# Three sets of key sums of a graph transformer's mixing part change place with the last qkv product

## The chip, the cores and the metric

The kernel runs on 1 core of a Trainium2 chip. The metric is the device time of one execution in microseconds. Where several runs are given, their median counts. The engines are PE (matmuls), DVE, ACT and POOL (elementwise work, POOL here above all as the issuer of scattering DMAs), and SP, which only issues DMAs.

## What is computed

A layer over a graph with 3125 nodes of 256 features: a layer norm, then a three-layer graph convolution and a mixing part side by side, their sum, and a feed-forward block for half of the nodes.

```python
xn = _layernorm(x)
x = x + gnn(xn, edge_index, ...) + mix(xn[None], ...)[0]
x = x + ffn(_layernorm(x)[None], ...)[0]
```

The change lies in the mixing part. With one position in the sequence its attention over the nodes comes down to elementwise work and small products:

```python
h = conv1d(logmap0(proj(x)), w_qkv)            # 256 -> 768 channels
t = logmap0(proj(expmap0(relu(batchnorm(h)))))
s = pointwise(depthwise(t))                    # "spread": 768 -> 768, groups of 32
q, k, v = split(concat(t, s))                  # per group of 96 channels
out = q * sum_over_group(k * v) / v            # "key sums" and quotients
ft = conv1d(out_on_the_ball, w_res) + b_res
```

The reference writes `vk = einsum(v, k)`, `out = einsum(vk, q)` and divides by the sum of `v`; for length 1 and 32 channels a group, a key sum of 32 channels is the only sum across channels in it.

## The kernel before

**Two parts that run against each other.** POOL issues 416 scattering DMAs (L763), four a row over 104 rows of edges, that build the matrix of edge counts in DRAM tile by tile. Meanwhile the other engines do the mixing part, in five chunks of 5 x 125 nodes (`NC` = 5, chunk `c`). Then PE begins with the first layer of the graph convolution. For each of 25 tiles SP waits until POOL's scatters for that tile have landed (`landed`), fetches the tile of counts into a ring of four slots (`fetch`), and PE multiplies it with the rows (`aggregate1`). POOL waits for the mixing part in some rows (`mixing_kept_up`: `qk_done` and `sq_done` by `KEYS_BY_ROW` and `SQUARES_BY_ROW`). Row 37 waits for the last key product of chunk 3.

**One turn of the mixing loop on PE** (L2452 to L2489, chunk `c`). The order is written out by hand; each engine works its own list in that order, and semaphores tie the lists together:

- first and second key sums of chunk `c`, with the output sums and residual products of chunk `c - 1` between and behind them (`outs`, `outs_turned`, `outs_rest`);
- six qkv products of chunk `c + 1`, `hidden(c + 1, m)` with `m` from 0 to 5. Each goes to one of two pairs of PSUM banks. ACT copies it out with a ReLU and squares it (L1821, L1814). From `m` = 2 on, a product waits until ACT has copied out the one two before it (`h_done`), so the last one, `m` = 5, waits for ACT's copy of 3. Behind products 3 and 5, `hidden` also issues a pair of norm sums over the squares (`norm_pair`);
- third and fourth key sums of chunk `c`, `key_sums(c, 2)` and `key_sums(c, 3)`, somewhere among the products;
- six spread products of chunk `c + 1`, `spread(c + 1, m)`, copied and squared by ACT (L1831, L1814), with norm sums between, then the last norm sums, ACT's copy of them (L1842) and their spread over the partitions (`norm_spread`).

A set of key sums is two matmuls with the block matrix `kones` into banks 6 and 7. The trace shows each fp32 matmul as two, so four in all. It waits for the product before it in the same banks (`qk_done`) and for ACT's copies of the spread (`s_evac`):

```python
def key_sums(c, n):
    ...
    for h in range(2):
        last = mm(bank(6 + h, 128, CH), kones[:, :], src[:, 2 + half, h * CH:(h + 1) * CH], True, True)
    last.then_inc(sem("k_done"), 1)
```

**Who waits for it.** DVE, in `key(c, n)` (L1219), multiplies q with the sums and signals `qk_done`. Its list for a chunk ends with: quotients of the second half (six elementwise passes, a reciprocal of 4.07 us, two more), `key(c, 3)`, `weigh(c, 2)`, `weigh(c, 3)`, then what `besides(c, 5)` puts there: one-hot batches for the node degrees in chunks 0 and 1, low halves of four weight pieces and twelve rows in chunk 3. The first key product of the next chunk follows. ACT squares the weighed outputs late, after its `veps_made` (`out_square`), and PE's output sums wait for that.

In the timelines, `psum<-big,wm` or `psum<-scr,wm` in f16 with x12 is a qkv product, in f32 spread products (x4 for one), `psum<-...,kones` key sums, `psum<-...,ones` with 128*32 norm sums (313 columns) or output sums (375 columns), `psum<-acc` bf16 degree batches, and `psum<-rows,scr` an aggregate of layer 1. L2164 is the helper that issues every matmul.

Of the kernel before, what the change touches and what calls it, by code (L numbers as in the profile page):

```python
# [144 lines left out]
def _build(ctx, nc, a, out, scratch):  # L145
# [7 lines left out]
    def sem(name):  # L153
        if name not in sems:
            sems[name] = ctx.enter_context(nc.semaphore(name))
        return sems[name]

    def milestone(name):

        if name in PE_MILESTONES:  # L160
            return sem("pe_milestones")
        return sem("act_milestones" if name in ACT_MILESTONES else "dve_milestones")
# [257 lines left out]
    def bank(b, p, n, o=0):  # L420
        return psum[:p, b, o:o + n]
# [1740 lines left out]
    def _(pe):  # L2162
        def mm(o, l, r, start, stop):
            return pe.matmul(o, l, r, start=start, stop=stop)  # L2164
# [31 lines left out]
        def degree(b):  # L2196
            ohp, oht = onehot[HOME[b]]
            pe.wait_ge(sem("onehot_done"), b + 1)
            if b == DEGREE_RUNS[0]:
                pe.wait_ge(sem("ft_done"), G)  # L2200
            for j in range(DB):
                last = mm(psum[TW * (j % 4):TW * (j % 4) + TW, 5, 0:P], oht[:, j // 2, :, j % 2],
                          ohp[:, j // 2, :, j % 2], b in (0, DEGREE_RUNS[0]) and j < 4,
                          b in (DEGREE_RUNS[0] - 1, sum(DEGREE_RUNS) - 1) and j >= DB - 4)
            last.then_inc(sem("degree_used"), 1)
# [79 lines left out]
        def bias_product():  # L2285
            pe.wait_ge(sem("layerw_loaded"), 48)
            pe.wait_ge(sem("cols_loaded"), 80)
            pe.wait_ge(sem("ft_done"), (NC - 1) * G)
            for k in range(8):
                last = mm(bank(5, P, D2), free(be1c[:, k:k + 1], 0, [[0, P]]), w2[:, k, :], k == 0, k == 7)  # L2290
            last.then_inc(milestone("be2w_done"), 1)

        def degrees_and_bounds():
            pe.wait_ge(sem("degree_kept"), 2)
            pe.wait_ge(milestone("squares_summed"), AFTER["squares_summed"])
            mm(bank(5, 128, 7, 16), ones[:, :], sums7, True, True).then_inc(milestone("bounds_done"), 1)
            mm(bank(5, P, T, 256), degree4, quarters, True, True).then_inc(milestone("degree_summed"), 1)
# [14 lines left out]
        def norm_spread(c):  # L2312
            pe.wait_ge(sem("norm_kept"), c + 1)
            pe.wait_ge(sem("s_evac"), c * NT + NT)
            pe.wait_ge(sem("sq_done"), c * 12 + 12)
            if c == 0:
                pe.wait_ge(sem("chosen_ready"), 4)
            for h in range(2):
                last = mm(bank(h, 128, CH), chosen[:, h, :], sums_kept, True, True)
            last.then_inc(sem("norm_spread"), 1)  # L2320

        def hidden(c, m):
            if m >= 2:
                pe.wait_ge(sem("h_done"), c * NT + (m - 1))
            elif c >= 1:
                pe.wait_ge(sem("row_kept"), c)
                pe.wait_ge(sem("s_evac"), c * NT + (m - 1))
                pe.wait_ge(sem("sq_done"), c * 12 + (m - 1))
                if c >= 2:
                    pe.wait_ge(sem("ft_done"), (c - 2) * G + 2 * m + 2)  # L2330
            for k in range(2):
                for hx, hw in ((0, 0), (1, 0), (0, 1)):
                    for h in range(2):
                        o = c * CW + h * CH
                        last = mm(bank(2 * (m % 2) + h, 128, CH), wq16[:, k, 1 - hw, m * 128:(m + 1) * 128],
                                  z16[:, k, hx, o:o + CH], k == 0 and (hx, hw) == (0, 0), k == 1 and (hx, hw) == (0, 1))
            last.then_inc(sem("qkv_done"), 1)
            if m in (3, 5):
                norm_pair(c, m // 2 - 1)
# [16 lines left out]
        def part_of(c, n):  # L2356
            return (hTs[c % 2], n) if n < 2 else (sTs[c % 2], n - 2)

        def key_sums(c, n):
            src, half = part_of(c, n)  # L2360
            pe.wait_ge(sem("qk_done"), c * 4 + n)
            if c == 0 and n == 0:
                pe.wait_ge(milestone("needs_ready"), AFTER["needs_ready"])
                pe.wait_ge(milestone("value_kept"), AFTER["value_kept"])
            if n >= 2:
                pe.wait_ge(sem("s_evac"), c * NT + n + 1)
# [3 lines that stand above are left out]
# [9 lines left out]
        def outs(c):  # L2379
            newest = min(c + 1, NC - 1)  # L2380
            pe.wait_ge(sem("osq_done"), c * 4 + 4)
            pe.wait_ge(sem("norm_kept"), newest + 1)
            for n in range(4):
                src, half = part_of(c, n)
                for h, (lo, hi) in enumerate(OUTS):
                    last = mm(quarter(2 * (n % 2) + h, 3 * P), ones[:, 0:32], src[:, 2 + half, lo:hi], n < 2, n >= 2)
            last.then_inc(sem("out_summed"), 1)
            pe.wait_ge(sem("o_done"), c * 4 + 4)
            pe.wait_ge(sem("row_kept"), newest + 1)
            pe.wait_ge(sem("s_evac"), newest * NT + NT)  # L2390
            pe.wait_ge(sem("sq_done"), newest * 12 + 12)
            if c >= 1:
                pe.wait_ge(sem("ft_done"), c * G)
            for j in range(AHEAD[c]):
                res(c, j)

        def outs_rest(c):

            for j in range(AHEAD[c], G):
                if j == 4 and c == 0:  # L2400
                    pe.wait_ge(sem("degree_kept"), 1)
                if j == 4 and c == 1:
                    pe.wait_ge(milestone("dinv_read"), AFTER["dinv_read"])
                    pe.wait_ge(milestone("bounds_read"), AFTER["bounds_read"])
                if j == 3 and c == NC - 1:
                    pe.wait_ge(milestone("be2w_read"), AFTER["be2w_read"])
                if j == 4 and c == NC - 1:
                    pe.wait_ge(sem("ft_done"), T - G + 1)
                res(c, j)

        def outs_turned(c):
            pe.wait_ge(sem("out_kept"), c + 1)
            for j in range(G):
                pe.transpose(bank(4, P, 1, 440 + j), umax_row[c % 2][:, j * P:(j + 1) * P], ident[0:1, 0:1])
            for j in range(G):
                o = j * P if j < 3 else j * P - OUTS[1][0]
                last = mm(bank(4, P, 1, 432 + j), outs_kept[:, o:o + P], chosen[:, j // 3, 0:1], True, True)
            last.then_inc(sem("out_turned"), 1)

        def degrees(c, at):  # L2420
            for b in range(*HALF_BATCHES[c][at]) if c < len(HALF_BATCHES) else ():
                degree(b)
# [29 lines left out]
        for c in range(NC):  # L2452
            key_sums(c, 0)
            if c >= 1:
                outs(c - 1)
            if c == 2:
                degrees_and_bounds()
            if c >= 1:
                outs_turned(c - 1)
            if c == 0:  # L2460
                for b in range(3, EARLY):
                    degree(b)
            key_sums(c, 1)
            if c >= 1:
                outs_rest(c - 1)
            degrees(c, 0)
            if c == NC - 1:
                key_sums(c, 2)
                bias_product()
                key_sums(c, 3)  # L2470
                break
            for m in range(NT):
                hidden(c + 1, m)
                if m == (0 if c else 3):
                    key_sums(c, 2)
                if m == 4 and c >= 1:
                    key_sums(c, 3)
                for b in range(*BETWEEN.get((c, m), (0, 0))):
                    degree(b)
            if c == 0:  # L2480
                key_sums(c, 3)
            spread(c + 1, 0, 3)
            if c == 0:
                degrees(c, 3)
            spread(c + 1, 3, NT)
            norm_pair(c + 1, 5)
            norm_spread(c + 1)
            degrees(c, 4)
            degrees(c, 5)  # L2489
# [363 lines left out]
```

## Time and profile before

| | |
|---|---|
| time, median of 3 runs | 1286.18 us (1285.31 to 1288.14) |
| the profiled execution | 1287.64 us, span 1285.8 us |
| PE busy | 1183.7 us (92%), 6591 matmuls |
| DVE busy | 732.1 us (57%) |
| POOL busy | 567.9 us (44%), 444.3 us of it in the 416 scatters |
| ACT busy | 478.9 us (37%) |
| granted clock of PE, mean | 0.979 |

The mixing loop lies between some 107 and 325 us of the span, layer 1 of the convolution from there to about 700 us, layers 2 and 3 behind it. POOL scatters from 95.85 us to 674 us. A row of a timeline gives the start, the time from the first start to the last end of what it merges, engine, line, operation, output and inputs, how many, and in brackets the idle time before it with what ended it. Rows of one engine can overlap a little, since a matmul's drain is in its duration. So the price of a piece of PE's list is read from start to start.

### The profile page before, as it was taken

How to read it: one execution, taken by the hardware profiler on the slowest of the kernel's cores; microseconds unless marked ns; L12 is line 12 of the kernel's file. 1: busy time of each engine (PE TensorE's matmuls, PEld its weight loads, DVE VectorE, ACT ScalarE, POOL GpSimd, SP SyncE). 2: the span in 40 equal slices, each digit the busy share in tenths (PEclk: the TensorE clock that was granted, in tenths of full speed). 3: DMA queues.
4: the chain of work that ended last, by engine and by line, in shares of the span. 5: the costliest groups of instructions: out<-in, count | busy, mean ns of one | idle time of the engine just before them, and what ended most of it. 6: DMA issues, size and time to landing. Idle time of an engine off the chain costs nothing.

```text
span 1285.8 us, 19145 instructions
## 1 busy us (share of the span) xinstructions
PE 1183.7 (92%) x6591; PEld 780.0 (61%) x6591; DVE 732.1 (57%) x1560; ACT 478.9 (37%) x1028; POOL 567.9 (44%) x580
## 2 busy tenths in 40 slices
PE   2998799889999999999979999999999899996995
PEld 2765456556665666666645666666666566653674
DVE  7878997779555455545523343333323388887253
ACT  4546873886432222223211123111111144441463
POOL 4108887777777777777773400440000000000633
PEclk9989898999999999999989999999999999998998
DMA  9882000004223221211314064333333266523201
GB/s 266 285 269 77 1 1 2 2 1 110 73 72 91 71 57 31 54 37 49 78 33 102 1 187 107 96 86 79 93 84 82 77 176 170 166 69 120 54 19 34
DMA packets 82939, 111.30 MB, mean 87 GB/s; under 512 B 51871, under 2 KB 67348, under 8 KB 82872
## 3 DMA queue, kind: packets, MB, share of 16 engines
q1 hardware_dynamic: 62344, 106.98, 30.2%
q0 software_dynamic: 20528, 3.47, 1.9%
q8 instruction: 37, 0.61, 0.2%
q14 instruction: 30, 0.25, 0.1%
HBM read 76.08 MB, written 27.67 MB: 81 GB/s over the span
## 4 chain that ended last, share of the span: by engine, by line
PE 48%; POOL 24%; issue 19%; DVE 6%; ACT 2%; DMA 1%; POOLq 1%; SPq 0%; DVEq 0%; ACTq 0%
PE psum L2164 47%; POOL counts L763 23%; ACT acc L1706 1%; POOLq L763 1%; DMA scr<-counts 0%; DVE scr L1562 0%; DVE big L965 0%; DVE scr L965 0%; DMA scr<-in_src_pad 0%; PE psum L2544 0%; DVE col L885 0%; POOL col L742 0%; PE psum L2702 0%; POOL out L822 0%; DVE big L958 0%
## 5 line engine op out<-in xcount | busy, mean ns | idle before, releaser
L763 POOL DMA_INDIRECT counts<-big,eidx x416 | 444.3, 1068 | 164.3 <-issue 127.9
L2164 PE MATMUL psum<-big,scr 125*125 125x512 f16 x1250 | 278.2, 382 | 7.2 <-DVE big L1362 6.5
L2164 PE MATMUL psum<-rows,scr 125*125 125x512 f16 x1250 | 274.6, 379 | 6.2 <-DMA scr<-counts 2.6
L2164 PEld LDWEIGHTS psum<-rows,scr 125*125 125x125 f16 x1250 | 170.1, 136 | 106.2 <-DMA scr<-counts 3.5
L2164 PEld LDWEIGHTS psum<-big,scr 125*125 125x125 f16 x1250 | 171.0, 138 | 104.6 <-DVE big L1362 7.0
L2164 PE MATMUL psum<-wb,scr 128*125 128x512 f16 x600 | 138.4, 382 | 2.4 <-DVE scr L1345 1.9
L2164 PEld LDWEIGHTS psum<-wb,scr 128*125 128x125 f16 x600 | 81.6, 137 | 48.3 <-issue 2.3
L815 POOL DMA_INDIRECT scr<-picked,eidx x13 | 22.9, 1758 | 181.0 <-issue 181.0
L1345 DVE TENSOR_TENSOR scr<-psum,scr 128x1000 f16<-128x1000 f32 x25 | 30.0, 1200 | 89.3 <-ACT scr L1989 89.1
L2164 PE MATMUL psum<-big,wm 128*128 128x313 f16 (+1 forms) x432 | 74.8, 324 | 3.1 <-ACT scr L1821 1.5
L1441 DVE SCALAR_TENSOR_TENSOR scr<-psum,col,wm 125x512 f32<-125x512 f32 x25 | 18.7, 749 | 98.8 <-PE psum L2164 98.8
L869 DVE BATCH_NORM_STATS2 col<-scr 125x6 f32<-125x512 f32 x75 | 49.5, 689 | 44.1 <-ACT scr L1998 28.1
L2164 PE MATMUL psum<-wa,scr 128*125 128x512 f16 x300 | 69.0, 379 | 2.4 <-DVE scr L1240 1.8
L804 POOL IOTA scr<- 125x63 f32 x1 | 0.2, 202 | 159.9 <-PE psum L2164 159.9
L2060 ACT ACTIVATE scr<-scr 125x512 f32<-125x512 f32 x25 | 15.7, 629 | 135.3 <-DVE scr L1441 135.3
L2164 PEld LDWEIGHTS psum<-big,wm 128*128 128x128 f16 (+1 forms) x432 | 47.7, 114 | 28.3 <-issue 5.4
L2164 PEld LDWEIGHTS psum<-wa,scr 128*125 128x125 f16 x300 | 40.6, 136 | 26.6 <-DVE scr L1240 2.7
L1989 ACT CAST scr<-psum 128x1000 f16<-128x1000 f32 x25 | 24.8, 992 | 70.2 <-PE psum L2164 56.2
L795 POOL TENSOR_SCALAR scr<-wa,col 128x512 f32<-128x512 f32 x4 | 6.3, 1587 | 100.9 <-DVE col L1467 100.6
L1993 ACT ACTIVATE big<-scr,col 125x512 f32 (+1 forms) x25 | 18.0, 722 | 80.4 <-DVE scr L1358 80.4
L1213 DVE RECIPROCAL scr<-scr 128x626 f32<-128x626 f32 x10 | 40.7, 4066 | 0.3
L822 POOL DMA_INDIRECT out<-rows,eidx x13 | 23.1, 1780 | 40.0 <-issue 30.6
(419 smaller groups left out, 1861.7 us busy)
## 6 DMA issues: line engine op xcount, KB each, us to landing
scr<-counts SPq DMA_DIRECT2D x75, 683.6 KB
counts<-wb SPq DMA_DIRECT2D x25, 683.6 KB
counts<-big,eidx POOLq DMA_INDIRECT x416
scr<-counts SPq DMA_DIRECT2D x75, 79.3 KB
scr<-in_x SPq DMA_DIRECT2D x25, 125.0 KB
picked<-big SPq DMA_DIRECT2D x5, 566.6 KB
rows<-in_x SPq DMA_DIRECT2D x5, 560.0 KB
out<-acc SPq DMA_DIRECT2D x5, 560.0 KB
```

Source lines behind the costliest of these rows:

```text
L763: pool.indirect_dma_start(cells, bass.IndirectOffsetOnAxis(ap=eidx[:, r * EQ + g:r * EQ + g + 1], axis=0), evalue[:, at_c:at_c + 1], None, ...
L815: pool.indirect_dma_start(got[:, g, :], None, picked_dram, bass.IndirectOffsetOnAxis(ap=picked[:, g:g + 1], axis=0), bounds_check=N - 1, o ...
L822: pool.indirect_dma_start(out, bass.IndirectOffsetOnAxis(ap=picked[:n, g:g + 1], axis=0), base[:n, g, :], None, bounds_check=N - 1, oob_is ...
L869: done.did(dve.bn_stats(st2[:, h, :], src[:, h * 512:(h + 1) * 512] if parts > 1 else src))
L1213: done.did(dve.reciprocal(tdiv, tdiv))
L1345: dve.tensor_tensor(xT16[:, 1].rearrange("p (b k) q -> p b (k q)", b=2), turned_halves(), xT16[:, 0].rearrange("p (b k) q -> p b (k q)", b ...
L1441: dve.scalar_tensor_tensor(out=pre[b][:, 0:D2], in0=bank(home, P, D2), scalar=d2out[:, bass.ds(t, 1)], in1=b2r, op0=ALU.mult, op1=ALU.add) ...
L1706: act.activation(zv[:, t, 0:D], x_rows[:, t, :], ACT.Identity, scale=z_scale[:, t:t + 1], bias=z_shift[:, t:t + 1]).then_inc(sem("z_done"), 1)
L1989: act.copy(xT16[:, 0].rearrange("p (b k) q -> p b (k q)", b=2), turned_halves()).then_inc(sem("xThi_done"), 1)
L1993: act.activation(h2in[:, t, 0, :], hbuf, ACT.Identity, scale=h2_scale[:, bass.ds(t, 1)]).then_inc(sem("hi2_done"), 1)
L2060: act.activation(pre[b][:, 0:D2], pre[b][:, 0:D2], ACT.Relu).then_inc(sem("relu2_done"), 1)
L2164: return pe.matmul(o, l, r, start=start, stop=stop)
```

## The change

In chunks 1, 2 and 3 `key_sums(c, 3)` moves from behind `hidden(c + 1, 4)` to behind `hidden(c + 1, 5)`, where chunk 0 has it already. In chunk 1 two degree batches (20 and 21) stood between the key sums and the last product; they now follow product 4 directly. Nothing is added or removed, and the lists of the other engines are untouched.

```diff
                 if m == (0 if c else 3):
                     key_sums(c, 2)
-                if m == 4 and c >= 1:
-                    key_sums(c, 3)
                 for b in range(*BETWEEN.get((c, m), (0, 0))):
                     degree(b)
-            if c == 0:
-                key_sums(c, 3)
+            key_sums(c, 3)
             spread(c + 1, 0, 3)
```

PE's list in chunk 1, from the product in front of the two changed places to the first spread products (here and below, `kones` are key sums, `acc` degree batches, `ones` norm sums, `wm` x12 a qkv product and `wm` x4 two spread products):

```order
 L2164 MATMUL psum<-acc 32x125 x32
 L2164 MATMUL psum<-big,wm 128x313 x12
-L2164 MATMUL psum<-scr,kones 128x313 x2
 L2164 MATMUL psum<-acc 32x125 x32
 L2164 MATMUL psum<-big,wm 128x313 x12
 L2164 MATMUL psum<-big,ones 32x313 x2
 L2164 MATMUL psum<-scr,ones 32x313 x2
+L2164 MATMUL psum<-scr,kones 128x313 x2
 L2164 MATMUL psum<-big,wm 128x313 x4
```

The key sums moved past two degree batches, the last product and the four matmuls of its norm sums.

PE's list in chunk 2 (chunk 3 reads the same but for the names of the buffers):

```order
-L2164 MATMUL psum<-big,wm 128x313 x12
-L2164 MATMUL psum<-scr,kones 128x313 x2
-L2164 MATMUL psum<-big,wm 128x313 x12
-L2164 MATMUL psum<-big,ones 32x313 x2
-L2164 MATMUL psum<-scr,ones 32x313 x2
+L2164 MATMUL psum<-big,wm 128x313 x24
+L2164 MATMUL psum<-big,ones 32x313 x2
+L2164 MATMUL psum<-scr,ones 32x313 x2
+L2164 MATMUL psum<-scr,kones 128x313 x2
 L2164 MATMUL psum<-scr,wm 128x313 x4
```

Products 4 and 5 now stand in a row (x24), their norm sums behind them, and the key sums last, right before the spread products.

## Rows read from the trace of the kernel before

**Rows 1.** the page's chain of waits, shares of the span by engine

```profile
PE 48%; POOL 24%; issue 19%; DVE 6%; ACT 2%; DMA 1%; POOLq 1%; SPq 0%; DVEq 0%; ACTq 0%
```

**Rows 2.** the chain in order of time: start us, us, what

```profile
638.24 0.13 POOL col L742
...
638.74 5.68 DMA scr<-counts
```

**Rows 3.** timeline of PE from 620: start, us, what [idle before <-releaser]

```profile
623.58 5.61 PE L2164 MATMUL psum<-rows,scr 125*125 125x512 f16 x25 [1.31 <-DMA scr<-counts]
...
644.46 5.61 PE L2164 MATMUL psum<-rows,scr 125*125 125x512 f16 x25 [1.25 <-DMA scr<-counts]
...
665.42 7.12 PE L2164 MATMUL psum<-big,scr 125*125 125x512 f16 x18 [6.51 <-DVE big L1362]
```

**Rows 4.** one stretch: us, busy us by engine (instructions), PEclk, DMA share, GB/s

```profile
402.00:622.00 220.00, 219.80 (x1099) 145.11 (x1099) 113.49 (x200) 61.18 (x107) 167.52 (x179) 1.00 0.22 54
```

**Rows 5.** timeline of PE, chunk 2

```profile
225.56 1.22 PE L2164 MATMUL psum<-scr,kones 128*128 128x313 f32 x4
228.23 1.79 PE L2164 MATMUL psum<-big,wm 128*128 128x313 f16 x12 [1.46 <-ACT scr L1821]
...
230.62 2.38 PE L2164 MATMUL psum<-scr,wm 128*128 128x313 f32 x8
...
240.42 0.46 PE L2164 MATMUL psum<-big,ones 128*32 128x313 f32 x2 [0.82 <-ACT scr L1814]
...
246.63 0.84 PE L2164 MATMUL psum<-big,ones 128*32 128x375 f32 x8 [2.56 <-ACT scr L1838]
```

**Rows 6.** timeline of ACT, chunk 2

```profile
227.32 0.86 ACT L1821 ACTIVATE scr<-psum,col 128x626 f32<-128x626 f32 x1
...
231.98 0.69 ACT L1831 ACTIVATE scr<-psum 128x626 f32<-128x626 f32 x1
```

**Rows 7.** timeline of all engines, chunk 0

```profile
125.55 1.32 PE L2164 MATMUL psum<-scr,kones 128*128 128x313 f32 x4
...
126.71 2.27 PE L2164 MATMUL psum<-scr,wm 128*128 128x313 f32 x8
...
127.96 0.69 ACT L1831 ACTIVATE scr<-psum 128x626 f32<-128x626 f32 x1 [1.53 <-PE psum L2164]
```

**Rows 8.** timeline of all engines, chunk 1

```profile
178.44 0.86 ACT L1821 ACTIVATE big<-psum,col 128x626 f32<-128x626 f32 x1
...
179.36 1.79 PE L2164 MATMUL psum<-big,wm 128*128 128x313 f16 x12
...
181.74 2.38 PE L2164 MATMUL psum<-big,wm 128*128 128x313 f32 x8
```

**Rows 9.** timeline of DVE, chunks 1 to 4

```profile
191.17 0.81 DVE L1197 SCALAR_TENSOR_TENSOR scr<-psum,scr 128x626 f32<-128x626 f32 x1
...
234.21 0.81 DVE L1197 SCALAR_TENSOR_TENSOR scr<-psum,scr 128x626 f32<-128x626 f32 x1
...
272.98 0.81 DVE L1197 SCALAR_TENSOR_TENSOR scr<-psum,scr 128x626 f32<-128x626 f32 x1
...
288.21 0.81 DVE L1197 SCALAR_TENSOR_TENSOR big<-psum,big 128x626 f32<-128x626 f32 x1 [6.06 <-PE psum L2164]
```

**Rows 10.** timeline of DVE, then of POOL

```profile
278.05 4.11 DVE L1197 SCALAR_TENSOR_TENSOR rows<-big,rows 125x256 f16<-125x256 f32 x12
...
278.62 4.38 POOL L763 DMA_INDIRECT counts<-big,eidx  x1 [0.31 <-issue]
...
320.66 0.97 POOL L763 DMA_INDIRECT counts<-big,eidx  x1 [0.70 <-issue]
```

**Rows 11.** stretches around two hand-overs, columns as in group 4

```profile
190.00:197.00 7.00, 3.82 (x69) 1.73 (x68) 5.88 (x8) 4.70 (x8) 5.48 (x6) 1.00 0.03 3
197.00:204.00 7.00, 6.34 (x38) 2.78 (x39) 4.63 (x15) 1.18 (x3) 5.68 (x6) 0.51 0.02 0
239.00:246.00 7.00, 3.72 (x24) 1.63 (x20) 1.82 (x3) 4.70 (x9) 5.29 (x8) 1.00 0.03 4
```

## The prediction

> **What bounds the kernel now.** I read the page's chain of waits first, then the chain in order of time. A quarter of the chain is POOL, almost all of it the 416 scatters at L763 [rows 1]. In order of time the chain leaves POOL at 638.24 us. SP then fetches a tile of counts, whose DMA runs from 638.74 for 5.68 us, and PE starts on it at 644.46 [rows 2, 3]. From there to the end PE carries most of the chain. So the instant that fixes the second half is 644.46, and two runners race for it: POOL, which scatters without pause, and PE, which comes out of the mixing part (the part that is changed) and then works through layer 1.
>
> The timeline of PE between 620 and 670 us says who loses. PE stood still for 1.31 us before 623.58 and for 1.25 us before 644.46, both times until a DMA of counts landed [rows 3]. Between 402 and 622 us PE was busy for 219.80 of 220.00 us [rows 4], so the lag with which it comes out of mixing is still there at 622. PE therefore has 1.31 + 1.25 = 2.56 us to spare at 644.46. **Up to 2.56 us that PE loses in mixing costs nothing, and nothing that PE wins there counts**, unless POOL's landings move too.
>
> POOL does have waits on the mixing part, so its slack must be read. The scatter row that waits for the last key product of chunk 3 starts at 320.66 [rows 10], while DVE starts that product at 272.98 [rows 9]. That is 47.7 us of slack, and no delay discussed here is near it.
>
> **What PE does at the changed places.** Take chunk 2. The key sums start at 225.56. Then PE is idle for 1.46 us and the last qkv product starts at 228.23, released by ACT [rows 5]: its semaphore asks for ACT's copy of product 3 (they count from 0), which runs from 227.32 for 0.86 us [rows 6]. The key sums fill a hole that ACT leaves anyhow. With them gone the hole is larger by their time, and the product starts where it started. So the product gains nothing. Chunk 3 repeats this 44.1 us later with the same 1.46 us. In chunk 1 the hole is filled: the product starts at 179.36, but ACT's copy of product 3 starts only at 178.44 and takes 0.86 us, so it is free at 179.30 [rows 8]. There too the product gains 0.06 us at most.
>
> **What the key sums cost in their new place.** They now stand between the norm sums behind the last product and the first spread product. The kernel before has this very order once, in chunk 0: key sums at 125.55, spread at 126.71 [rows 7]. That is 1.16 us for one set, with its weight loads. In chunks 1 to 3 PE goes from that spread to the last norm sums without a hole (230.62 to the one before 240.42 in chunk 2, which ACT ends [rows 5]), so the 1.16 us isn't filled up on PE. What could swallow part of it is ACT, which copies the first spread. In chunk 2 the copy starts at 231.98 with no idle time before it [rows 6], 1.36 us after the spread, so ACT is just not waiting. In chunk 0 the copy starts 127.96 - 126.71 = 1.25 us after the spread [rows 7]. In the new order the spread of chunk 2 starts at 230.62 + 1.16 = 231.78 and the copy at 233.03, so 1.05 us late. A chunk thus loses between 1.05 and 1.16 us. All that follows to the hand-over of the chunk (the last squares, the sums, their spread, the output sums that wait until 246.63) hangs on this pair of engines and moves with it. **Three chunks: 3.15 to 3.48 us, taken as 3.3.**
>
> **Does the later key sum hold up DVE?** k_done now comes when the moved sums end, 1.32 us after their start [rows 7]. Chunk 1: 181.74 + 1.32 = 183.06 [rows 8], and DVE takes that key product at 191.17 [rows 9], behind quotients and one-hot batches. No wait. Chunk 2: 230.62 + 1.32 = 231.94, DVE at 234.21 [rows 5, 9]. Covered with 2.3 us. Chunk 3: 44.1 us after chunk 2, at 276.04, against 272.98 before: **here DVE waits 3.1 us.** Queued behind it are two weighings, the four low weight pieces and twelve rows (the block at 278.05, 4.11 us [rows 10]). Behind that DVE sat idle for 6.06 us before 288.21, until PE's first key sums of chunk 4 [rows 9]. 3.1 fits into 6.06, so it costs nothing. If that cover were gone it would cost up to 3.1 us. POOL's wait on it has the 47.7 us named above.
>
> **The sum.** Work added or removed: none. PE leaves mixing 3.3 us late. It keeps this lag through layer 1, where its waits before 622 us are for engines that follow it. Of the lag 1.31 is swallowed at 623.58 and 1.25 at 644.46: 3.3 - 2.56 = 0.7. With the ends of the terms it is 0.6 to 0.9; I take 0.8, nearer the price of the chunk-0 row, which is the same piece of order. The next wait, 6.51 us before 665.42, is for DVE's rows that come out of PE's own product after 644.46 [rows 3], so it moves along. The profiled execution took 1287.64 us for a span of 1285.8; it would become 1288.4. It lies 1.46 above the median of the three runs, 1286.18, on which I build: **1287.0 us**, +0.06%. A measurement of this kernel can tell about 0.2% (2.6 us) from no change.
>
> **Rivals.**
> 1. *No trace at all.* PE's clock was granted at 1.00 from 190 to 197 us, with PE busy for 3.82 of 7.00 us, and at 0.51 (1.2 GHz, the lower of its levels) in the 7 us behind [rows 11]. Busy 6.34 us at 0.51 is work of some 3.3 us, so this fall costs about 3.0 us. The change moves work by about 1.1 us against it. If the fall stays away, PE's lag is 3.3 - 3.0 = 0.3 and POOL's landing decides as before: 1286.2. PE alone could then be at most 2.56 - 0.3 = 2.3 us earlier, and only if POOL too came earlier by as much.
> 2. *Slower, by the clock.* The hand-over from chunk 2 to 3 looks much like that first one: 3.72 us busy from 239 to 246, yet the clock stayed at 1.00 [rows 11]. In the new order it comes 2.2 us later. If the clock falls there as it did at 197, the price is another 3.0: 3.3 + 3.0 - 2.56 = 3.7, so 1289.9. It decides from the point where the lag exceeds 2.56 + 2.6 us. Against it: the holes of both late hand-overs passed at full clock. The Trainium skill, "TensorE: Matmul & The Clock Gate", section on the HAM clock gate, says that the throttled clock is the default and that activity releases it, which makes the wider hole before the last product (2.6 us instead of 1.46) a risk too; by that rule alone the change would lose in three more places. The trace shows holes of 2.56 us, as before 246.63 [rows 5], with the clock at 1.00, so here it is no more than a chance.
> 3. *The spare time isn't there.* One scatter took 4.38 us at 278.62 where its neighbours take 1.3, just under DVE's block of twelve rows at 278.05 [rows 10]. The change moves that block by 2.2 + 3.1 = 5.3 us against POOL. If a scatter slips in between the rows, POOL is up to 3.4 us earlier, the two waits for landings vanish, and the whole 3.3 is paid: 1289.5. If two are caught, POOL is later and the end with it, by less than that. The Trainium skill, "SBUF — State Buffer", section "SBUF: two separate sides", says that DVE and GpSimd share one port pair as an exclusive lock, taken by whoever starts first, and that DMAs issued from GpSimd starve for it. By that rule the block catches one scatter wherever it lands, or misses by a hair; the trace agrees with the long scatter, and no row shows how often it misses.
> 4. *Faster.* It needs rival 1 and an earlier POOL together, and even then gives 2.3 us, under the bound. Only with noise on top does it pass 0.2%.
> 5. *The change does nothing.* Excluded by the order: the two matmuls stand elsewhere in three chunks.
>
> **How the numbers follow.** Forecast (1286.8 to 1287.1 before noise) 0.60. Rival 1: 0.15. Rival 2: 0.11. Rival 3: 0.10, half of it above the bound of 0.2%. Rival 4: 0.04. Within 0.2%: 0.60 + 0.15 + 0.05 = 0.80. Slower: 0.11 + 0.05 = 0.16. Faster: 0.04. The three runs before spread from 1285.3 to 1288.1, which the range must carry under the forecast and rival 1. Above, it reaches to rivals 2 and 3: 1285.2 to 1289.9.
>
> **What would show it.** In the trace after: the last product starts at the same distance from ACT's copy of product 3, with an idle of about 2.6 us before it in chunks 2 and 3. The key sums follow, and the first spread starts 1.16 us later in each of three chunks. DVE idles some 3 us before the last key product of chunk 3 and that much less before chunk 4. PE enters layer 1 about 3.3 us later, and its two waits for counts shrink to nothing. The forecast is wrong if the lag at layer 1 is under 2 or over 4.5 us, if the granted clock falls somewhere new, or if PE still waits over 0.5 us for counts.

## The result, and the profile after

**The kernel after is slower, and slower than the prediction's range.** Over six runs each: after 1293.22 us median (1289.50 to 1296.17), before 1287.21 (1285.31 to 1288.14), ratio 1.0047 with a 95% interval of 1.0033 to 1.0061. That is 4 to 8 us, where 0.8 was forecast. The profiled execution of after is the lowest of its runs: 1289.50 us, span 1287.7, mean granted clock 0.975 against 0.979. Its trace therefore shows less than the usual loss.

The page's chain of waits has lost its POOL part, [rows 1] had 24% there:

```profile
PE 80%; DVE 10%; ACT 5%; issue 2%; DMA 2%; POOL 0%; DVEq 0%; SPq 0%; ACTq 0%; POOLq 0%
```

Below, product 4 and product 5 are the last two of the six qkv products, and the hand-over to a chunk is the stretch between its first and second set of key sums, in which the output sums of the chunk before it are made. Timeline of PE in chunks 2 and 3, in layer 1 and behind it, after:

```profile
223.01 1.79 PE L2164 MATMUL psum<-big,wm 128*128 128x313 f16 x12
227.32 1.79 PE L2164 MATMUL psum<-big,wm 128*128 128x313 f16 x12 [2.51 <-ACT scr L1821]
...
230.86 2.27 PE L2164 MATMUL psum<-scr,wm 128*128 128x313 f32 x8
...
268.16 1.79 PE L2164 MATMUL psum<-big,wm 128*128 128x313 f16 x12
272.46 2.70 PE L2164 MATMUL psum<-big,wm 128*128 128x313 f16 x12 [2.51 <-ACT big L1821]
...
277.57 2.28 PE L2164 MATMUL psum<-big,wm 128*128 128x313 f32 x8
...
309.69 1.32 PE L2164 MATMUL psum<-scr,kones 128*128 128x313 f32 x4 [1.29 <-DVE big L1197]
...
645.78 5.56 PE L2164 MATMUL psum<-rows,scr 125*125 125x512 f16 x25
...
666.44 7.08 PE L2164 MATMUL psum<-big,scr 125*125 125x512 f16 x18 [6.26 <-DVE big L1362]
...
760.96 1.52 PE L2164 MATMUL psum<-wc,scr 128*125 128x256 f16 x12 [0.87 <-DMA scr<-scr]
```

The kernel before has this row where after has the one at 309.69:

```profile
305.30 1.32 PE L2164 MATMUL psum<-scr,kones 128*128 128x313 f32 x4 [1.29 <-DVE big L1197]
```

Chunk 2 is what the prediction drew: a hole of 2.51 us, product 5 in 1.79 us, 7.85 us from product 4 to the first spread product (before 6.69, so 1.16 more). Chunk 3 has the same hole, but behind it product 5 takes longer, and from product 4 to the spread it is 277.57 - 268.16 = 9.41 us, **1.56 more than in chunk 2**. The windows say why (start and end us, length, busy us of PE, its weight loads, DVE, ACT and POOL with their instructions, then the granted clock and the DMA's share and rate), after first, then before:

```profile
272.00:276.00 4.00, 3.54 (x20) 1.59 (x20) 1.08 (x2) 3.42 (x5) 3.08 (x4) 0.64 0.02 2
...
292.00:296.00 4.00, 2.51 (x16) 0.59 (x16) 3.93 (x6) 3.50 (x7) 3.39 (x3) 0.70 0.02 0
```

```profile
272.00:276.00 4.00, 3.67 (x25) 2.24 (x26) 3.90 (x6) 3.90 (x6) 3.12 (x3) 1.00 0.02 2
...
292.00:296.00 4.00, 4.00 (x22) 3.14 (x19) 3.96 (x3) 3.97 (x10) 3.20 (x5) 1.00 0.01 0
```

The granted clock is 0.64 and 0.70, a mix of 1.2 and 2.4 GHz, in two stretches where the kernel before has 1.00. The second lies in the hand-over to chunk 4, behind a hole of 2.56 us that both orders have. On the other hand the fall of [rows 11] at 197 us is gone in this execution. At 309.69 PE is 4.39 us behind before (305.30). At 645.78 1.32 us of this are left ([rows 3]: 644.46), at 666.44 1.02, and PE no longer waits for counts. A wait of 0.87 us for a transposing DMA at 760.96, where before had none, doubles that, and the span ends 1.9 us later.

### The profile page after: what moved, and what is told of

Read it like the earlier page. It is cut to its first block, busy times and chain, and to the rows that moved or that the text cites. A ratio compares the mean times of both kernels' runs of the same rounds, so it can differ in the third digit from the quotient of the medians.

```text
span 1287.7 us, 19145 instructions
## 1 busy us (share of the span) xinstructions
PE 1185.4 (92%) x6591; PEld 780.4 (61%) x6591; DVE 731.5 (57%) x1560; ACT 479.1 (37%) x1028; POOL 567.8 (44%) x580
## 4 chain that ended last, share of the span: by engine, by line
PE 80%; DVE 10%; ACT 5%; issue 2%; DMA 2%; POOL 0%; DVEq 0%; SPq 0%; ACTq 0%; POOLq 0%
PE psum L2164 78%; PE psum L2541 2%; DVE acc L944 1%; DMA scr<-scr 1%; DVE scr L1197 1%; DVE scr L1213 1%; DVE big L1197 1%; ACT acc L1706 1%; DMA scr<-picked,eidx 1%; ACT scr L1989 0%; PE psum L2534 0%; ACT scr L1831 0%; DVE acc L946 0%; ACT scr L1857 0%; DVE big L965 0%
## 5 line engine op out<-in xcount | busy, mean ns | idle before, releaser
L1441 DVE SCALAR_TENSOR_TENSOR scr<-psum,col,wm 125x512 f32<-125x512 f32 x25 | 18.6, 749 | 98.8 <-PE psum L2164 98.8
```

Of the source, the lines that this page charges most:

```text
L1441: dve.scalar_tensor_tensor(out=pre[b][:, 0:D2], in0=bank(home, P, D2), scalar=d2out[:, bass.ds(t, 1)], in1=b2r, op0=ALU.mult, op1=ALU.add) ...
```

## The experiments

**Two theories.** A, the clock: the wider holes before product 5 make PE's granted clock fall, and each fall is paid because the lag is already beyond the cover. B, the lag: the later key sums cost 1.16 us a chunk or more, further down too, and the falls are incidental. The kernel that tells them apart keeps the new order and puts matmuls whose result nobody uses into the two holes ("filled" below; an idle time of 1.40 us is left, about the 1.46 of before). All experiments but the unchanged ones are edits of one loop.

**The conditions.** In 16 of the 18 runs the kernel before, timed beside them, took 1455 to 1467 us and not 1288. The engines, PE above all, stood still there for longer in front of instructions for which the profile names no releaser. It reads as if the instructions themselves came late, which no run shows. The same kernel after, its PE weight loads' idle time in the view of waits (total us, times, longest), then the stretch from 140 to 180 us, first in the profiled execution above, then in f1_after:

```profile
PEld psum L2164 <- issue: 51.7, 140, 1.8
...
140.00:180.00 40.00, 32.27 (x346) 21.54 (x344) 35.63 (x49) 31.99 (x82) 32.31 (x29) 0.87 0.02 2
```

```profile
PEld psum L2164 <- issue: 111.7, 259, 2.6
...
140.00:180.00 40.00, 24.06 (x150) 10.35 (x153) 18.95 (x21) 12.68 (x22) 24.49 (x25) 0.66 0.02 1
```

PE began 150 matmuls against 346 in these 40 us. It stood still for 15.9 us of them in f1_after, 12.3 without a releaser; the program is also at a later place in after by then. What brings this about is open. It is not the chip: it struck five chips, and h1_before to h3_late had it on the same one as i1_after and i2_fill, half an hour apart from them, had not. Two runs, i1_after and i2_fill, met the conditions of the result and decide on time. The others are used for what their traces show at product 5, and only weakly for time: there POOL has no share in the page's chain, so no lag is covered, and the intervals are 0.3 to 0.5% to each side.

### The order of after with filled holes: e1_fill, f2_fill, g1_fill, i2_fill

Against after (the kernel has the loop in a helper, here it is written out):

```diff
             for m in range(NT):
                 hidden(c + 1, m)
...
+                if m == 4 and c >= 2:
+                    for _ in range(5):
+                        mm(bank(5, 128, 128, 300), kones[:, :], ident[:, :], True, True)
...
             key_sums(c, 3)
```

> The new order, with five idle 128x128 matmuls (result unused, kones by ident, into a spare place of bank 5) between products 4 and 5 of chunks 2 and 3, where the kernel after lets PE stand for 2.51 us. They fill the hole and leave the order and its lag as they are. Theory A (clock): the wider holes make the granted clock fall more often, in the profiled execution of after at 274 us and then at 294; most of the 6 us are such falls. Filled, the fall at 274 goes, and the time is before plus 1 to 3 us (lag 3.3 less the 2.56 of cover, and what is left of the falls). Theory B (lag): PE's list simply comes late and the late start is paid in full or more downstream; the filler changes nothing, before plus 6 us.

> The new order with the holes of 2.51 us before product 5 of chunks 2 and 3 filled with five matmuls of unused result, as in e1_fill. Where before takes some 1287 us, theory A (clock): before plus 1 to 3 us, no clock fall between 265 and 290 us. Theory B (lag): before plus 6 us, as f1_after.

> The same kernel as e1_fill and f2_fill (new order, holes of 2.51 us in chunks 2 and 3 filled with matmuls of unused result), on its own. The question is first whether before takes 1287 us or 1455 us beside it. At 1287: theory A (clock) before plus 1 to 3 us, theory B (lag) before plus 6 us, the loss of after. At 1455: PE is held up for want of instructions in the mixing part, the holes are elsewhere, and neither theory expects more than 4 us.

> The new order with filled holes once more. If before takes 1287 us beside it: theory A (clock) 1288 to 1290, 3 to 5 us under the kernel after; theory B (lag) the same as after, 1293. If before takes 1455 to 1470 us again: product 5 at 1.79 us in both chunks by theory A, and a time between those of before and after.

### The kernel after once more: f1_after, h2_after, i1_after

> The kernel after once more, unchanged, to have its time beside the experiments and a second trace of it. On a chip where before takes some 1287 us: both theories 1291 to 1295; theory A (clock): granted clock 0.004 to 0.006 under that of before in the timed executions and, in the trace, the falls at 272 and 292 us again or others in the mixing part. Theory B (lag): the clock is as in before and the lag at layer 1 is over 4 us all the same. On a chip like that of the first four experiments (before 1456 us, PE held up for want of instructions) POOL ends no chain, so no lag is covered: before plus 3 to 6 us by either.

> The kernel after, unchanged. So far the traces of the new order show product 5 longer than 2.3 us (full clock: 1.79) in 6 of the 7 places where a hole of over 2.1 us stands before it, and in none of the 15 places with a narrow or filled hole. Theory A (clock): the product is slowed again in chunks 2 and 3 wherever the hole is over 2.1 us. From product 4 to the first spread product it then takes 9.3 to 9.5 us in place of 7.85. Time: before plus 2 to 6 us, if PE's want of instructions leaves such holes. Theory B (lag): 7.85 us in both chunks, and all of the time's loss is the order's 1.16 us per chunk: before plus 3.3.

> The kernel after once more. If before takes 1287 us beside it: after 1291 to 1296 by both theories; theory A (clock) expects in its trace one fall of the clock more than in the profiled execution, at the hand-over from chunk 1 to 2 or before product 5 of chunk 2, in executions that take 1293 us. If before takes 1455 to 1470 us again: two more holes before product 5, slowed (over 2.0 us in place of 1.79) by theory A where they are over 2.1 us wide.

**Measured, i1_after and i2_fill** (same chip, one comparison, before 1288.01 us median): after 1291.79 us, ratio 1.0029 (1.0017 to 1.0040); filled 1286.70 us, ratio 0.9993 (0.9981 to 1.0006). The loss is there again and **filling the holes takes all of it away, 5.1 us between the medians**, although the key sums still stand late and PE executes 20 matmuls more. Theory A expected 1288 to 1290 for the filled kernel, theory B 1293: it came in under both, far nearer to A.

The scatter of the 7 and 12 executions puts 3.1 to 6.4 us around the difference of the means, 4.8 us (an estimate from their times). The granted clock says the same for all of them and not only for the profiled ones: 0.9749 on average in after, 0.9787 filled, 0.9774 in the 18 of before. 0.0038 of 1290 us are 4.9 us (an estimate), so the clock is the size of the whole difference. Late instructions are not: PE's own idle time without a releaser is 1.6 us in before, after, i1_after and i2_fill alike.

The traces show where, PE in i1_after (its profiled execution is the highest of its 7, 1293.68 us):

```profile
224.92 1.79 PE L2164 MATMUL psum<-big,wm 128*128 128x313 f16 x12
229.22 2.39 PE L2164 MATMUL psum<-big,wm 128*128 128x313 f16 x12 [2.51 <-ACT scr L1821]
...
234.34 2.27 PE L2164 MATMUL psum<-scr,wm 128*128 128x313 f32 x8
...
273.29 1.79 PE L2164 MATMUL psum<-big,wm 128*128 128x313 f16 x12
277.59 2.93 PE L2164 MATMUL psum<-big,wm 128*128 128x313 f16 x12 [2.51 <-ACT big L1821]
...
282.74 2.27 PE L2164 MATMUL psum<-big,wm 128*128 128x313 f32 x8
...
314.77 1.32 PE L2164 MATMUL psum<-scr,kones 128*128 128x313 f32 x4 [1.29 <-DVE big L1197]
...
671.53 6.98 PE L2164 MATMUL psum<-big,scr 125*125 125x512 f16 x18 [6.27 <-DVE big L1362]
...
707.86 7.08 PE L2164 MATMUL psum<-wb,scr 128*125 128x512 f16 x24 [1.89 <-DVE scr L1345]
```

and in i2_fill:

```profile
224.72 1.79 PE L2164 MATMUL psum<-big,wm 128*128 128x313 f16 x12
226.35 1.28 PE L2164 MATMUL psum<-ident,kones 128*128 128x128 f32 x10
229.03 1.79 PE L2164 MATMUL psum<-big,wm 128*128 128x313 f16 x12 [1.40 <-ACT scr L1821]
...
232.58 2.27 PE L2164 MATMUL psum<-scr,wm 128*128 128x313 f32 x8
...
269.88 1.79 PE L2164 MATMUL psum<-big,wm 128*128 128x313 f16 x12
271.50 1.28 PE L2164 MATMUL psum<-ident,kones 128*128 128x128 f32 x10
274.18 1.79 PE L2164 MATMUL psum<-big,wm 128*128 128x313 f16 x12 [1.40 <-ACT big L1821]
...
277.73 2.27 PE L2164 MATMUL psum<-big,wm 128*128 128x313 f32 x8
...
309.84 1.32 PE L2164 MATMUL psum<-scr,kones 128*128 128x313 f32 x4 [1.29 <-DVE big L1197]
...
666.60 5.87 PE L2164 MATMUL psum<-big,scr 125*125 125x512 f16 x18 [6.26 <-DVE big L1362]
...
701.82 5.39 PE L2164 MATMUL psum<-wb,scr 128*125 128x512 f16 x24 [1.89 <-DVE scr L1345]
```

From product 4 to the first spread product it is 9.42 and 9.45 us in i1_after, 7.86 and 7.85 in i2_fill: each fall costs 1.6 us. The product starts 4.30 or 4.31 us after product 4 in both kernels; the filler moves nothing, it only keeps PE at work. The clock of 272 to 280 us, i1_after first:

```profile
272.00:276.00 4.00, 3.08 (x26) 1.53 (x23) 3.97 (x2) 3.62 (x12) 3.09 (x4) 1.00 0.02 2
276.00:280.00 4.00, 2.41 (x11) 1.47 (x12) 2.17 (x3) 3.75 (x6) 3.09 (x4) 0.76 0.01 0
```

```profile
272.00:276.00 4.00, 2.60 (x23) 1.78 (x26) 2.76 (x3) 3.94 (x8) 3.09 (x4) 1.00 0.01 0
276.00:280.00 4.00, 4.00 (x24) 2.32 (x28) 1.97 (x3) 2.91 (x5) 3.09 (x4) 1.00 0.02 0
```

The end of mixing (309 to 315 us) comes 314.77 - 309.84 = 4.9 us apart: 1.6 + 1.6 for the two products, and 1.6 for the hand-over to chunk 3, where i1_after has a fall and i2_fill none. In the hand-over to chunk 4 both have one (12.12 and 12.20 us in place of 10.57). At 666 us it is still 4.9. Two stages behind it are 1.1 and 1.7 us shorter in the filled kernel (the last two rows of each; before has the long form at 701.89 too); 0.9 of that is lost at once to a wait for DVE. 4.9 + 1.1 + 1.7 - 0.9 = 6.8, the difference of the spans (1291.9 and 1285.1). So of this one pair 4.9 us come out of mixing, and 1.9 lie in stages whose clock happened to fall otherwise; no hole of the change is near them.

**Measured, the others.** Filled: 1.0018 (0.9986 to 1.0050), 1.0009 (0.9976 to 1.0042), 1.0011 (0.9981 to 1.0041). After: 0.9986 (0.9946 to 1.0027), 1.0014 (0.9985 to 1.0044). Where before takes 1455 us and more, neither differs measurably from it. The 3 to 6 us that f1_after's expectation named are not confirmed, and only half excluded. But their traces have the falls: product 5 takes 3.28 us in chunk 3 of f1_after and 3.32 and 2.08 us in chunks 2 and 3 of h2_after. It is slowed in none of the six places of the three filled ones. In two of these, chunk 2 of e1_fill and of f2_fill, product 4 was late and no wide hole would have stood there, so four of the six test the filler.

### Before, only chunk 1, only chunks 2 and 3: h1_before, e2_only1, j4_only1, e3_only23, f3_only23, j1_only23

Against before:

```diff
-                if m == 4 and c >= 1:
+                if m == 4 and c >= 1 and c not in (2, 3):    # (1,) for "only chunk 1"
                     key_sums(c, 3)
...
-            if c == 0:
+            if c == 0 or c in (2, 3):                        # (1,)
                 key_sums(c, 3)
```

> The kernel before, unchanged, for a trace of it under the conditions of these runs (some 1455 us), and as a test of the comparison with itself: ratio 1 within its interval. Theory A (clock): product 5 of chunks 2 and 3 stands behind holes of at most 1.9 us and takes 1.79 us in both, the duration at full clock. Theory B (lag) has no view of that.

> Only chunk 1 has the new order; there the place in front of product 5 is filled by degree batches in either order, so no hole grows. Theory A (clock): within 1 us of before, unless the hand-over from chunk 1 to 2, where the clock of before is at 0.51 from 197 to 204 us, keeps its clock as it did in the profiled execution of after; then PE enters layer 1 some 2 us earlier and POOL's landings hold the time where it was. Theory B (lag): 1.1 us of lag is under the 2.56 us of cover, so 0; if instead every chunk's move costs alike, before plus 2 us.

> Only chunk 1 in the new order, where no hole grows, beside a before of some 1288 us. Both theories: 1.16 us of lag under the cover: within 1 us of before. If it were over 2 us slower, chunk 1 would carry a part of the loss that neither explains.

> Only chunks 2 and 3 have the new order; both get the hole of 2.51 us. Theory A (clock): both wide holes are there, so most of the loss is: before plus 4 to 6 us, with the clock falling between 270 and 300 us. Theory B (lag): 2.3 us of lag is under the 2.56 us of cover, so 0 to 0.5 us; if every chunk's move costs alike, before plus 4 us.

> Only chunks 2 and 3 in the new order, as in e3_only23. Where before takes some 1287 us, theory A (clock): before plus 3 to 6 us, with falls of the clock between 265 and 300 us. Theory B (lag): 2.3 us of lag is under the 2.56 us of cover, so 0 to 0.5 us.

> Only chunks 2 and 3 in the new order, beside a before of some 1288 us. Theory A (clock), with the sizes of the second trace of after (1.55 us per slowed product 5, 1.5 us per slowed hand-over behind it): lag 2 x 1.16 + 2 x 1.55 + up to 2 x 1.5, less the 2.6 to 3.1 us of cover: before plus 3 to 5 us. Theory B (lag alone): 2.3 us, less than the cover: before plus 0 to 0.5 us.

**Measured.** Before against itself 0.9989 (0.9963 to 1.0016). Only chunk 1: 1.0006 (0.9973 to 1.0039) and 1.0021 (0.9989 to 1.0052). Only chunks 2 and 3: 1.0034 (0.9998 to 1.0071), 1.0015 (0.9970 to 1.0059), 1.0015 (0.9978 to 1.0052). All three of the latter lean to the slow side and none is measurable alone; as times they settle nothing. The traces do. f3_only23 in chunk 3, and h1_before in chunk 3:

```profile
345.27 2.36 PE L2164 MATMUL psum<-big,wm 128*128 128x313 f16 x12 [2.51 <-ACT big L1821]
```

```profile
343.67 1.79 PE L2164 MATMUL psum<-big,wm 128*128 128x313 f16 x12
...
347.97 1.79 PE L2164 MATMUL psum<-big,wm 128*128 128x313 f16 x12 [1.45 <-ACT big L1821]
```

### Late matmuls without a wide hole: e4b_lag, f4_lag, j2_lag

Against before (again written out):

```diff
             if c == 0:
                 key_sums(c, 3)
+            if c >= 2:
+                for _ in range(8):
+                    mm(bank(5, 128, 128, 300), kones[:, :], ident[:, :], True, True)
             spread(c + 1, 0, 3)
```

> The order of before, its holes as narrow as they were (1.46 us), and eight idle 128x128 matmuls (result unused) behind the last product's norm sums in chunks 2 and 3, some 1.7 us each: a lag of about 3.4 us without a wide hole. Theory A (clock): the lag less the cover, before plus 0.8 to 2 us. Theory B (lag): the same loss as after, before plus 6 us.

> The order of before with 2 x 1.7 us of matmuls of unused result behind product 5 of chunks 2 and 3, as in e4b_lag. Where before takes some 1287 us, theory A (clock): before plus 0.8 to 2 us, clock as in before. Theory B (lag): before plus 6 us, as f1_after.

> The order of before with 2 x 1.7 us of matmuls of unused result behind product 5 of chunks 2 and 3, beside a before of some 1288 us. Theory A (clock): a lag of 3.4 us with narrow holes, so before plus 0 to 1 us, like the filled kernel. Theory B (lag): the loss of after, plus 4 to 6 us.

**Measured.** 1.0052 (1.0021 to 1.0083), 1.0033 (0.9994 to 1.0072), 0.9991 (0.9951 to 1.0031). Inconclusive between the theories: a lag of 3.4 us without any cover is 0.23%, and 6 us are 0.41%; of the three intervals the first two hold both and the last holds only the smaller. Product 5 ran in 1.79 us in all six places, so none of them has a fall there. This never ran beside a before of 1288 us.

### The key sums later still: h3_late, j3_late

Against after:

```diff
-            key_sums(c, 3)
+            if c == 0:
+                key_sums(c, 3)
...
             spread(c + 1, 3, NT)
+            if c >= 1:
+                key_sums(c, 3)
             norm_pair(c + 1, 5)
```

> The key sums of chunks 1 to 3 moved still further back, behind the last spread product's norm sums and before the last norm sums, where PE waits 0.82 us for ACT in any case. The hole of 2.51 us before product 5 stays, but the spread products no longer start 1.16 us late. Theory A (clock): product 5 of chunks 2 and 3 is slowed as in the kernel after; before plus 2 to 4 us. Theory B (lag): only some 0.4 us of lag per chunk is left; no difference to before.

> The key sums behind the last spread product, holes of 2.51 us before product 5 and 0.4 us of lag per chunk, beside a before of some 1288 us. Theory A (clock): two to four falls of 1.5 us each, 3 to 6 us, plus 1.2, less 3 us of cover: before plus 1 to 4 us. Rival C, from the earlier trace of this kernel, in which both products 5 ran at full clock behind holes of over 2.5 us: the hole alone does not do it, and the time is that of before.

**Measured, a miss for all.** 1.0080 (1.0044 to 1.0115) and 1.0162 (1.0112 to 1.0212): 12 and 24 us, far more than any theory had. In h3_late mixing isn't where they go. The stretches to 400 and to 550 us and PE's idle time without a releaser, h1_before and then h3_late:

```profile
0.00:400.00 400.00, 291.04 (x1857) 182.11 (x1858) 262.65 (x444) 202.17 (x396) 223.04 (x232) 0.88 0.28 81
0.00:550.00 550.00, 397.72 (x2329) 249.32 (x2329) 316.02 (x542) 237.04 (x465) 306.73 (x320) 0.86 0.25 72
...
PE psum L2164 <- issue: 29.0, 40, 2.3
```

```profile
0.00:400.00 400.00, 297.44 (x1863) 186.16 (x1864) 264.73 (x447) 201.93 (x396) 219.72 (x225) 0.87 0.28 82
0.00:550.00 550.00, 399.01 (x2303) 248.39 (x2304) 311.28 (x534) 235.34 (x463) 304.37 (x315) 0.85 0.25 72
...
PE psum L2164 <- issue: 47.6, 47, 6.7
```

At 400 us PE has begun 1863 matmuls against 1857; at 550 us, in layer 1, 2303 against 2329, and over the whole span it stood without a releaser for 18.6 us longer. Why this order brings it about wasn't taken apart; as a time the experiment says nothing on the two theories. Against the simplest form of theory A, that every wide hole brings a fall, stands what PE did in h3_late:

```profile
347.18 1.79 PE L2164 MATMUL psum<-big,wm 128*128 128x313 f16 x12 [2.51 <-ACT big L1821]
```

Behind holes of 2.89 and 2.51 us both products ran at full clock. A wide hole alone is not enough.

### Product 5 in all traces

| before product 5 of chunks 2 and 3 | places | longer than 1.79 us |
|---|---|---|
| idle 2.20 to 2.89 us, key sums moved away | 15 | 12 |
| idle of at most 1.83 us (before's order, filled, or narrow by chance) | 25 | 0 |

The 15 are: both places of after, i1_after, h2_after, e3_only23, f3_only23 and h3_late, and chunk 3 of f1_after, j1_only23 and j3_late. The three at full clock are chunk 2 of after and both of h3_late. The table counts every trace, before's own included. One of the 12 doesn't belong to its hole: in chunk 2 of e3_only23 product 4 already took 3.32 us, behind a wait of 4.74 us, and the clock stayed at 0.50 through the 2.23 us before product 5. So 11 of 14 places lost the clock in the hole itself. Against them stand the six filled places with the same 4.30 us from product 4 to product 5 (both of g1_fill and i2_fill, chunk 3 of e1_fill and f2_fill): none of the six was slowed. The hand-over to chunk 4, whose hole is 2.56 us in either order, slowed its output sums in 9 of 13 traces with chunk 3 in the new order and in 2 of 7 in the old one, the hand-over to chunk 3 in 8 of 13 and in 3 of 7: a lean, not a proof. A slowed product 5 is not what it needs: of the 9, 5 followed one (of 8 slowed) and 4 did not (of 5), and three of the four filled kernels are among these 4.

## Why the prediction was wrong

**The sum for the order was right.** 1.05 to 1.16 us a chunk: product 4 to the first spread product went from 6.69 to 7.85 us, 1.16, with the clock undisturbed. That is the upper end of the range, 3.48 us for three where 3.3 was taken. The product itself gained nothing: it starts 4.30 or 4.31 us after product 4 in before, after and filled alike, with 2.51 us of idle time in after where 2.6 was forecast.

**DVE's part was right.** It waited before the last key product of chunk 3 (after):

```profile
277.84 0.81 DVE L1197 SCALAR_TENSOR_TENSOR scr<-psum,scr 128x626 f32<-128x626 f32 x1 [4.76 <-PE psum L2164]
...
290.96 0.81 DVE L1197 SCALAR_TENSOR_TENSOR big<-psum,big 128x626 f32<-128x626 f32 x1 [3.95 <-PE psum L2164]
```

4.76 us in place of 3.1, the slowed product being in it, and the idle time behind it shrank from 6.06 ([rows 9]) to 3.95. It cost nothing. In chunks 1 and 2 there was no wait.

**The cover was right, and a little larger.** 4.39 us at 309.69 became 1.32 at 645.78: 3.07 us swallowed against 2.56 forecast, the rest in small pieces. i1_after lost 9.47 us in mixing and was 6.40 late at 650.86, again 3.07 less.

**The step that failed is the discount on the clock.** The sum has no term for a fall of the clock. The prediction named "the wider hole before the last product (2.6 us instead of 1.46)" as a risk and set it aside: "The trace shows holes of 2.56 us, as before 246.63 [rows 5], with the clock at 1.00, so here it is no more than a chance." (It also counted three more places; the hole grows in two, since chunk 1's is filled.) One kind of place that passed in one trace is not a measure of the risk. In 11 of 14 places PE lost the clock in such a hole, at 1.56 to 1.60 us each where it was measured beside a clean one, and with the holes filled the loss was gone. The Trainium skill, "TensorE: Matmul & The Clock Gate", section "HAM oscillation — how this bites in real kernels", describes PE throttled again and again because it waits between short bursts. The slowed products agree with it in kind, 2.39 and 2.93 us in place of 1.79 in i1_after; its example has waits of 3 to 5 us, wider than these holes, so it points this way without giving the odds. The same page of the Trainium skill, section "Part 1: The HAM clock gate (the "warmup" mystery)", says that one kernel's slow start differs in length from run to run. That is about the start of a kernel, but chunk 2, slowed in i1_after (2.39 us) and not in after (1.79), agrees with it.

**What the falls cost.** The lag of i1_after, step by step: order 3 x 1.16 = 3.48; product 5 twice, 1.57 + 1.60; the hand-overs to chunks 3 and 4, 12.22 and 12.12 us between their two sets of key sums instead of 10.57, so 1.65 + 1.55. The sum is 9.85 against 9.47 measured, the difference being where it entered chunk 1. Less 3.07: 6.4, and the span ends 6.1 later. Without the two products it would be 3.2 less, without the hand-overs as much again, and 3.48 - 3.07 = 0.4 is left. That is a little under the forecast of 0.6 to 0.9, and the filled kernel's interval (-2.4 to +0.8 us) holds both 0.4 and most of that range. That the two slowed products come from the hole is shown by filling it. The hand-overs stay open: they fell in the old order and in filled kernels too, so of what is left beyond the order's 0.4 us, 3.2 have a shown cause and 3.2 only a lean. Nor does one execution, the slowest of its seven, say how the median loss of 6.0 us in the result is made up.

**The rivals.** "No trace at all" had its condition met: the fall at 197 us was absent in the profiled execution of after. It gave back 2.7 us (the hand-over took 8.40 us instead of 11.12), and this only made the lowest of six runs, since new falls took more. "Slower, by the clock" was the right mechanism and put the time at 1289.9; it had one fall of 3.0 us in the hand-over to chunk 3, where there were up to four of 1.6, two of them before product 5. A chance of 0.11 was far too low. "The spare time isn't there" rests on an error: POOL did come 3.4 us earlier in after (634.83, [rows 2] 638.24; why wasn't taken apart), and that can't make anything slower. PE's waits in before are time it lost there; a lag of L ends up as L - 2.56 whether POOL is earlier or not. The scatter didn't slip: one of 4.38 us stood under DVE's twelve rows again, at 283.48.

**The conditions named beforehand** did their work. The lag at layer 1 was 4.39 us in after, just under the limit of 4.5, and 9.47 us in i1_after, and the granted clock fell somewhere new, at 272 and 292 us in after.

## What to carry to other kernels

A wait that another engine imposes is not free room: what PE does in it may be what keeps its clock up, so moving work out of a hole is costed with the clock falling behind it, at the price of a fall read from the same trace, unless many holes of that width are seen to pass. If such a piece must move, a few matmuls of unused result in its place are a cheap test. Here they gave the whole loss back, and no more: the filled kernel was not measurably faster than before. And work out a lag against the waits of the kernel before: an engine that becomes early can't take cover away.

## What was not expected of the hardware

- The same program took 1288 us or 1455 to 1467 us, by conditions of the run that stayed unknown, with PE's weight loads idle without a releaser for 111.7 us instead of 51.7. In the slower ones intervals of 0.3 to 0.5% to each side hid a change of that size.
- A fall of the clock costs about 1.6 us behind a hole of 2.5 us, half of the 3.0 that the fall at 197 us had led to expect.
- One transposing DMA differed from execution to execution. In after it ran from 751.53 for 9.38 us (first fence, the chain in order of time) and PE waited for it. In before it was issued at 750.56 and released ACT at 758.29, so some 7.7 us (second fence, SP's queue, ACT, PE), and PE came at 758.95 without a wait. In i1_after it took 8.84 us. The extra 1.7 us in after, and not PE's lag, made the wait of 0.87 us, which is half of what after's span lost.

```profile
751.53 9.38 DMA scr<-scr
```

```profile
750.56 1.93 SPq L601 DMA_TRANSPOSE scr<-scr  x1
...
758.29 0.63 ACT L1973 ACTIVATE scr<-scr 125x512 f16<-125x512 f32 x1 [3.68 <-DMA scr<-scr]
...
758.95 1.48 PE L2164 MATMUL psum<-wc,scr 128*125 128x256 f16 x12
```
